# A selective scan, a router, experts and attention on one core: rows read by two kinds of products, unread products placed by a count of work, and a first unit over two queues

## Time and profile before

| | |
|---|---|
| three runs | 1349.19, 1353.96, 1361.01 us (median 1353.96) |
| profiled execution | 1352.84 us, span 1351.4 us |
| mean granted PE clock | 0.875 |
| busy | PE 1197.1 (89%), DVE 781.7 (58%), ACT 513.1 (38%), POOL 314.5 (23%) |
| DVE scans (L1194) | 256, busy 571.5 us |

### The profile page before, as it was taken

One profiled execution on the slowest core, in us unless ns is written; L12 is line 12 of the kernel. 1 busy time (PEld: TensorE's weight loads), 2 busy tenths in 40 slices (PEclk: granted clock), 3 DMA queues, 4 the chain that ended last, 5 costly groups with the idle time before them and its releaser, 6 DMA issues.

```text
span 1351.4 us, 30014 instructions
## 1 busy us (share of the span) xinstructions
PE 1197.1 (89%) x12231; PEld 774.1 (57%) x12231; DVE 781.7 (58%) x926; ACT 513.1 (38%) x1328; POOL 314.5 (23%) x941
## 2 busy tenths in 40 slices
PE   2689898989889899998988499999999598999998
PEld 1555455555545555554554377777777455565665
DVE  5587979699998787978996211121211365542211
ACT  4465556476764655644653111111111111221110
POOL 2043424234334342423323211111111200000000
PEclk9976779589997777957896599999999798999999
DMA  6364846425363153532312562222210300000000
GB/s 177 48 171 88 209 78 157 110 29 139 55 133 69 33 130 45 100 69 48 67 33 91 204 231 99 95 98 94 97 43 16 114 27 0 0 5 11 16 16 16
DMA packets 182202, 110.22 MB, mean 82 GB/s; under 512 B 92285, under 2 KB 176640, under 8 KB 179712
## 3 DMA queue, kind: packets, MB, share of 16 engines
q1 hardware_dynamic: 178176, 99.37, 30.0%
q0 software_dynamic: 3456, 8.48, 1.9%
q10 hardware_dynamic: 432, 0.46, 0.1%
HBM read 63.38 MB, written 43.90 MB: 79 GB/s over the span
## 4 chain that ended last, share of the span: by engine, by line
PE 68%; DVE 13%; ACT 7%; issue 7%; POOL 2%; DMA 2%; SPq 1%; DVEq 0%; POOLq 0%; ACTq 0%
PE psum L1497 10%; PE psum L1509 10%; DVE h L1194 10%; PE psum L2009 8%; PE psum L891 8%; PE psum L877 6%; ACT decay L1026 4%; PE psum L2020 4%; PE psum L858 4%; PE psum L845 3%; PE psum L1952 2%; PE psum L924 2%; PE psum L1944 1%; PE psum L1996 1%; PE psum L901 1%
## 5 line engine op out<-in xcount | busy, mean ns | idle before, releaser
L1194 DVE TENSOR_TENSOR_SCAN h<-decay,psum 128x1024 f32<-128x1024 f32 x256 | 571.5, 2273 | 111.0 <-ACT psum L1036 91.2
L1026 ACT ACTIVATE decay<-psum 128x512 f32<-128x512 f32 x512 | 278.4, 597 | 183.0 <-PE psum L858 181.8
L877 PE MATMUL psum<-xdiag,bstat 96*128 96x64 bf16 x4096 | 199.1, 210 | 17.6 <-DVE h L1194 16.4
L858 PEld LDWEIGHTS psum<-rows,shared 12*128 12x128 bf16 x4096 | 89.9, 103 | 175.5 <-issue 121.8
L877 PEld LDWEIGHTS psum<-xdiag,bstat 96*128 96x128 bf16 x4096 | 165.5, 109 | 38.0 <-DVE h L1194 23.6
L891 PE MATMUL psum<-h,cstat 128*32 128x512 f32 x1024 | 172.8, 756 | 1.2 <-DVE h L1194 1.0
L858 PE MATMUL psum<-rows,shared 12*128 12x64 bf16 x4096 | 123.5, 205 | 23.0 <-DMA rows<-parts_d 14.9
L1497 PE MATMUL psum<-xdt,shared 128*128 128x320 f32 x512 | 141.5, 438 | 0.7 <-ACT xdt L1556 0.7
L1509 PE MATMUL psum<-shared,hid 128*128 128x256 f32 x640 | 139.5, 379 | 0.6 <-ACT hid L1550 0.6
L1353 POOL TENSOR_TENSOR carry<-decay,h 128x16 f32<-128x16 f32 x240 | 58.0, 242 | 335.0 <-ACT decay L1026 334.3
L1509 PEld LDWEIGHTS psum<-shared,hid 128*128 128x128 f32 x640 | 121.0, 190 | 17.2 <-issue 1.1
(11 more groups left out here) (237 smaller groups left out, 1152.6 us busy)
## 6 DMA issues: line engine op xcount, KB each, us to landing
shared<-in_w SPq DMA_DIRECT2D x16, 1024.0 KB, 4.8
xdiag<-x_parts_d SPq DMA_DIRECT2D x128, 96.0 KB
x_parts_d<-x_parts SPq DMA_DIRECT2D x16, 384.0 KB, 3.8
x_parts_d<-x_parts SPq DMA_DIRECT2D x24, 256.0 KB, 3.1
rows<-parts_d SPq DMA_DIRECT2D x128, 48.0 KB
disp_d<-r_xl SPq DMA_DIRECT2D x4, 1305.0 KB, 7.9
xd<-disp_d SPq DMA_DIRECT2D x8, 652.5 KB, 6.3
picked_d<-r_xl SPq DMA_DIRECT2D x4, 1024.0 KB, 5.3
```

What stands on the lines that cost most here:

```text
L858: ins = pe.q.matmul(bank_a[half][:, i * T:(i + 1) * T], s["astat"][strip, RCH * g + q, :], rows[strip, c % 2, q, :], start=True, stop=True)
L877: ins = pe.q.matmul(to.rearrange("p d (s e) -> p s d e", e=2), bstat[0:ROWS, c % 2, b, :], xdiag[0:ROWS, c % 2, b, :, d, :], start=True, s ...
L1026: act.q.activation(decay[:, gi % NB, 8 * half:8 * half + 8, :], per_d(bank_a[half]), ACT.Exp).then_inc(sem("exp"), 1)
L1194: dve.q.tensor_tensor_scan(out=h[:, half_slot(c, half), ch:ch + G, :].rearrange("p d t -> p (d t)"), data0=decay[:, gi % NB, :, :].rearran ...
```

## The change

- `astat`, `rows`: the decay products read all 32 rows of their strip in place of 12. The other 20 rows are zeros, written by two new memsets on POOL in the prologue; the loads of `astat` wait for one, the first `rows` load for the other.
- The input products read 128 rows in place of 96; the upper 32 rows of `bstat` and `xdiag` are zeros that the old memsets write.
- Unread products: `unread_after` counts for each group what PE does beside decays and inputs, in products of 512 columns (`PE_WORK`), and gives each group what it lacks of three. They now multiply `bstat` and `xdiag` (512 columns, 128 rows) from group 2 on: 85 groups get three, 7 get one, 162 none; 262 in all, 48 of them in the first 32 groups.
- 14 unread products after the last router product, and 16 after the last expert product, ahead of the second layer.
- The first unit: A's middle and low parts come ahead of other work on ACT and DVE. SP stores B's parts first. ACT issues the middle and low stores of x, and, after all stores of x have landed, the loads of chunk 0's `xdiag`. SP issues the load of the second unit's tokens between chunk 0's and chunk 1's `rows` loads, no longer in the scan.

```diff
@@ prologue, on_sp
             sp.wait_ge(sem("a_parts_st"), 16)
+            sp.wait_ge(sem("astat_zero"), 1)
             for g in range(ROWG):
...
-            sp.wait_ge(sem("u_dthi"), 1)
-            store_dt(k, s, 0, 0)
-            sp.wait_ge(sem("x_hi"), 1)
-            store_x(k, s, 0, 0)
             sp.wait_ge(sem("u_blo"), 1)
             for j in range(3):
-                store_b(k, s, 0, j)
+                store_b(k, sp, s, 0, j)
+            sp.wait_ge(sem("u_dthi"), 1)
+            store_dt(k, sp, s, 0, 0)
+            sp.wait_ge(sem("x_hi"), 1)
+            store_x(k, sp, s, 0, 0)
             sp.wait_ge(sem("u_dtmid"), 1)
-            store_dt(k, s, 0, 1)
-            sp.wait_ge(sem("u_xmid"), 1)
-            store_x(k, s, 0, 1)
+            store_dt(k, sp, s, 0, 1)
             sp.wait_ge(sem("u_dtlo"), 1)
-            store_dt(k, s, 0, 2)
-            sp.wait_ge(sem("u_xlo"), 1)
-            store_x(k, s, 0, 2)
+            store_dt(k, sp, s, 0, 2)
             sp.wait_ge(sem("bstat_zero"), 1)
-            sp.wait_ge(sem("xdiag_zero0"), 1)
+            sp.wait_ge(sem("rows_zero"), 1)
             sp.wait_ge(sem("st_dt"), DT_ST)
             sp.wait_ge(sem("st_b"), B_ST)
-            load_rows(k, s, 0, LOADS[0])
+            load_rows(k, sp, s, 0, LOADS[0])
+            sp.q.dma_start(ux[:, :, :], x_in[:, UT:2 * UT, :]).then_inc(sem("u_ld"), 16)
+            load_rows(k, sp, s, 1, LOADS[0])
             sp.wait_ge(sem("st_x"), X_ST)
-            load_rows(k, s, 0, LOADS[1] + LOADS[2])
             sp.wait_ge(sem("xdiag_zero1"), 1)
-            load_rows(k, s, 1, sum(LOADS, ()))
+            load_rows(k, sp, s, 1, LOADS[1] + LOADS[2])
@@ prologue, on_pool
             pool.q.memset(s["x_parts"][:, :, :].bitcast(F32), 0.0).then_inc(sem("words_zero"), 1)
+            pool.q.memset(s["astat"][:, :, :].bitcast(F32), 0.0).then_inc(sem("astat_zero"), 1)
             pool.q.memset(s["bstat"][:, :, :, :].bitcast(F32), 0.0).then_inc(sem("bstat_zero"), 1)
+            pool.q.memset(s["rows"][:, :, :, :].bitcast(F32), 0.0).then_inc(sem("rows_zero"), 1)
@@ prologue, on_act
             act.q.copy(x_part[1], s["x_f"]).then_inc(sem("u_xmid"), 1)
+            act.wait_ge(sem("u_xmid"), 1)
+            store_x(k, act, s, 0, 1)
+            act.wait_ge(sem("u_xlo"), 1)
+            store_x(k, act, s, 0, 2)
             act.wait_ge(sem("p_c"), 1)
             act.q.copy(s["cmat"][:, 0, :], bank_c[:, 0:CSPAN]).then_inc(sem("c_taken"), 1)
+            act.wait_ge(sem("xdiag_zero0"), 1)
+            act.wait_ge(sem("st_x"), X_ST)
+            load_rows(k, act, s, 0, LOADS[1] + LOADS[2])
             both_sd(1, late)
@@
+IDLE_ROUTED, IDLE_PLACED = 14, 16
+def unread_products(pe, ident, bank, n):
+    for _ in range(n):
+        pe.q.matmul(bank, ident[:, :], ident[:, :].unsqueeze(1).broadcast_to([P, 4, P]), start=True, stop=True)
...
-AWAKE = (2, 3, 6, 0)
+PE_WORK = {"y": 4, "u_turn": 4, "u_proj": 6, "u_dt": 4, "u_tx": 4, "tr": 2, "yT": 4, "proj": 4}
...
+def unread_after(schedule):
+    work, gi = [0] * (TOTAL + LAG), 0
+    for kind, *x in schedule:
+        if kind == "stream":
+            gi = x[0]
+        elif kind == "y_sel" and x[0] == CHUNKS - 2:
+            break
+        work[gi] += PE_WORK.get(kind, 0)
+    return [max(0, 3 - w) for w in work]
@@ selective_scan, on_pe
-            def stay_awake(bank):
-                pe.wait_ge(sem("tri"), 1)
-                for _ in range(2):
-                    pe.q.matmul(bank, tri[:, 1, :], tri[:, 1, :].unsqueeze(1).broadcast_to([P, 4, P]), start=True, stop=True)
+            def stay_awake(c, n):
+                pe.wait_ge(sem(f"tokens_ld{c % 2}"), TOKENS_LD * (c // 2 + 1))
+                for _ in range(n):
+                    pe.q.matmul(bank_a[1], bstat[:, c % 2, 0, :], xdiag[:, c % 2, 0, 0:2, :, :].rearrange("p k d e -> p (k d e)"),
+                                start=True, stop=True)
...
-                if j in AWAKE and gi > GROUPS * CPB // 4 + 1:
-                    stay_awake(bank_a[1])
+                if gi >= 2:
+                    stay_awake((gi - 1) // GROUPS, unread[gi - 2])
...
-                        strip = slice(32 * g, 32 * g + PAIR_ROWS)
+                        strip = slice(32 * g, 32 * (g + 1))
...
-                        ins = pe.q.matmul(to.rearrange("p d (s e) -> p s d e", e=2), bstat[0:ROWS, c % 2, b, :],
-                                          xdiag[0:ROWS, c % 2, b, :, d, :], start=True, stop=True)
+                        ins = pe.q.matmul(to.rearrange("p d (s e) -> p s d e", e=2), bstat[:, c % 2, b, :],
+                                          xdiag[:, c % 2, b, :, d, :], start=True, stop=True)
...
+            unread_products(pe, ident, bank_y, IDLE_ROUTED)
@@ second_layer, on_pe
         pe.wait_ge(sem("w_rest"), all_weights)
+        pe.wait_ge(sem("evac7"), k.products[7])
+        unread_products(pe, ident, bank_kv[1], IDLE_PLACED)
```

More of the change, by code:

```diff
@@ L187, with load_rows @@
 LOADS = ((("dt", 0), ("dt", 1), ("dt", 2), ("dt", 3), ("b", 0), ("b", 1)), (("x", 0), ("x", 1)), (("x", 2), ("x", 3)))
-def load_rows(k, s, c, piece):
+def load_rows(k, q, s, c, piece):
     buf, t = c % 2, slice(c * T, (c + 1) * T)
@@ L198, in load_rows, with store_dt @@
             src = s["parts_d"][:, :, RCH * n:RCH * (n + 1), t].rearrange("k h p t -> (k h) p t")
-            k.sp.q.dma_start(s["rows"][32 * n:32 * n + PAIR_ROWS, buf, :, :], src).then_inc(rows_ld, 16)
+            q.q.dma_start(s["rows"][32 * n:32 * n + PAIR_ROWS, buf, :, :], src).then_inc(rows_ld, 16)
         elif what == "x":
-            k.sp.q.dma_start(s["xdiag"][2 * PAIR_ROWS * n:2 * PAIR_ROWS * (n + 1), buf, :, n].rearrange("r b d e -> r b (d e)"),
+            q.q.dma_start(s["xdiag"][2 * PAIR_ROWS * n:2 * PAIR_ROWS * (n + 1), buf, :, n].rearrange("r b d e -> r b (d e)"),
                              x_src[n]).then_inc(x_ld, 16)
         else:
-            k.sp.q.dma_start(s["bstat"][n:ROWS:DH, buf, :, STATE * n:STATE * (n + 1)], b_src).then_inc(x_ld, 16)
+            q.q.dma_start(s["bstat"][n:ROWS:DH, buf, :, STATE * n:STATE * (n + 1)], b_src).then_inc(x_ld, 16)
 ROWS_LD, TOKENS_LD = 16 * ROWG, 16 * (S // 2 + DH)
 B_ST, DT_ST, X_ST = 16 * 3, 16 * 5, 16 * 5
-def store_dt(k, s, u, j):
+def store_dt(k, q, s, u, j):
     m, n = MOVED[j]
@@ L215, in store_dt, with store_b, store_x @@
     if n == 1:
-        k.sp.q.dma_start(s["parts_d"][m, :, :, t].rearrange("h p t -> p h t"), s["dt_parts"][j]).then_inc(k.sem("st_dt"), 16)
+        q.q.dma_start(s["parts_d"][m, :, :, t].rearrange("h p t -> p h t"), s["dt_parts"][j]).then_inc(k.sem("st_dt"), 16)
         return
     for dh in range(DH):
-        k.sp.q.dma_start(s["parts_d"][m:m + n, dh, :, t].rearrange("m p t -> p m t"),
+        q.q.dma_start(s["parts_d"][m:m + n, dh, :, t].rearrange("m p t -> p m t"),
                          s["dt_parts"][j][:, dh, :].unsqueeze(1).broadcast_to([P, n, UNIT])).then_inc(k.sem("st_dt"), 16)
-def store_b(k, s, u, j):
+def store_b(k, q, s, u, j):
     m, n = MOVED[j]
     dst = s["b_parts_d"][UNIT * u:UNIT * (u + 1)].rearrange("(i p) m n -> p i m n", p=P)
-    k.sp.q.dma_start(dst[:, :, m:m + n, :], s["b_parts"][:, :, 0:n, :]).then_inc(k.sem("st_b"), 16)
-def store_x(k, s, u, j):
+    q.q.dma_start(dst[:, :, m:m + n, :], s["b_parts"][:, :, 0:n, :]).then_inc(k.sem("st_b"), 16)
+def store_x(k, q, s, u, j):
     m, n = MOVED[j]
@@ L234, in store_x @@
     if n == 1:
-        k.sp.q.dma_start(dst[:, :, m, :], s["x_words"][j]).then_inc(k.sem("st_x"), 16)
+        q.q.dma_start(dst[:, :, m, :], s["x_words"][j]).then_inc(k.sem("st_x"), 16)
         return
     for i in range(2):
-        k.sp.q.dma_start(dst[:, i, m:m + n, :], s["x_words"][j][:, i, :].unsqueeze(1).broadcast_to([P, n, 2 * D])
+        q.q.dma_start(dst[:, i, m:m + n, :], s["x_words"][j][:, i, :].unsqueeze(1).broadcast_to([P, n, 2 * D])
                          ).then_inc(k.sem("st_x"), 16)
@@ L350, in on_act @@
             act.q.copy(a_part[0], a_sb[:, :, :]).then_inc(sem("a_hi"), 1)
+            act.wait_ge(sem("a_rest"), 1)
+            act.q.copy(a_part[1], a_rest[:, :, :]).then_inc(sem("a_mid"), 1)
             act.wait_ge(sem("p_delta"), 1)
             act.q.copy(s["delta"], bank_delta[:, 0:UNIT]).then_inc(sem("p_delta_out"), 1)
-            act.wait_ge(sem("a_rest"), 1)
-            act.q.copy(a_part[1], a_rest[:, :, :]).then_inc(sem("a_mid"), 1)
             act.wait_ge(sem("p_b"), 1)
@@ L430, in on_dve @@
             dve.q.tensor_tensor(a_rest[:, :, :], a_sb[:, :, :], a_part[0], ALU.subtract).then_inc(sem("a_rest"), 1)
-            dve.wait_ge(sem("x_ld_late"), 32)
-            moments(range(UT, 6))
             dve.wait_ge(sem("a_mid"), 1)
@@ L435, in on_dve @@
             dve.q.tensor_tensor(a_part[2], a_rest[:, :, :], a_part[1], ALU.subtract).then_inc(sem("a_lo"), 1)
+            dve.wait_ge(sem("x_ld_late"), 32)
+            moments(range(UT, 6))
             dve.wait_ge(sem("b_hi"), 1)
@@ L554, in unit_steps @@
 def unit_steps(u):
```

(15 more changed lines are left out.)

## The result

The changed kernel takes **1272.84 us** (median of 4 runs, 1271.40 to 1277.38) where the kernel before takes 1357.49 (4 runs, 1349.19 to 1369.98): ratio 0.9401, 95% interval 0.9342 to 0.9461. The forecast was 1254 us, range 1238 to 1290. Ratios and intervals, here and in the table, take only runs within 1.5% of the fastest of the same kernel (of these eight, 1369.98 us stands outside), while medians take all of them, so that a ratio isn't the quotient of the two medians. The profiled execution is the slowest of the four, 1277.38 us with a span of 1276.0.

What follows compares the result with a forecast made beforehand. In the scan, DVE bounds at full clock and PE at half clock. Gains 84.0 - 5 + 5.5 + 12 + 3.5 = 100 us off the profiled 1352.84 give 1252.8; with 1.1 for the median, 1254 us, range 1238 to 1290.

Steps and rivals of the forecast that it cites:

- The rows count: PE's clock: products count with their rows, zeros included, so wider operands hold it; 0.68 with the ring hidden.
- Wider operands: Decays of 32 rows, inputs of 128, and their two memsets on POOL: cost 0 us.
- From group 32 on: Scan's other 224 groups: 84.0 us gained at full pace, less 5 for unread products and short falls.
- 224 x 2.294: Scan from group 32: 224 groups at the full-clock pace of 2.294 us, taken from 597.8, leaving 84.0 us.
- my allowance of 5 for relapses and the ring: Scan from group 32: 2 us for unread products, decays and exponentials waiting in turn, 3 for short clock falls.
- the 515 that I named as a sign: Sign that the forecast holds: the stretch from group 32 to the scan's end takes near 515 us.
- The first 32 groups: Start of the scan, 94.5 us: gain 5.5 from the earlier ux load and 12 of 15.6 from the clock.
- The start: Before the first scan: reordered stores and loads gain 3.5 us, bounds 0 and 5.
- The idle stretches: Unread products before experts and second layer: gain 0, bound 3 us each, as the clock falls again before work.
- Loop: Rival, 0.12: clock holds, but three unread products, decays and exponentials set their groups' pace; 13.6 us, total 1266.
- A: Rival, 0.13: rows don't count, only the unread products' placing works; half the low time stays, total 1297 us.
- C: Rival, 0.05: slower; groups with y products from 32 on lose the pair ahead, clock stays low, 1536 us.

Runs made afterwards that it cites:

- e2: Changed kernel with decays of 12 rows and inputs of 96 again, unread products in the new places: 1422.94 us, ratio 1.044 to the kernel before.
- e4: Changed kernel without unread products in the scan; wide operands and the idle stretches' products stay: 1275.34 us, ratio 0.944 to the kernel before.
- f4: Changed kernel with astat's memset halved, first unit on SP's queue, old unread pairs in the scan, none in the idle stretches: 1269.23 us.
- e5: Changed kernel with the memset of astat in two halves, the second behind DVE's first operations: 1273.11 us, ratio 0.937 to the kernel before.
- f3: The changed kernel measured again, unaltered, in a later batch: 1276.82 us, ratio 0.940 to the kernel before.
- e1: Changed kernel with wide rows kept but the scan's unread products in their old places: 1270.06 us, ratio 0.941 to the kernel before.
- f2: Changed kernel with astat's memset halved, first unit on SP's queue, and the scan's unread products in their old places: 1265.94 us, ratio 0.931.
- f1: Changed kernel with astat's memset in two halves and the first unit on SP's queue alone: 1268.30 us, ratio 0.933 to the kernel before.
- e7: Changed kernel with the first unit's x stores and xdiag loads back on SP's queue, which also reorders them: 1274.23 us, ratio 0.938.
- e6: Changed kernel without the 14 and 16 unread products in the two idle stretches: 1282.84 us, ratio 0.943 to the kernel before.

## Why the prediction was right, and where it was off

The direction, the mechanism and the range held; the profiled execution was put at 1252.8 us and took 1277.38, 24.6 more. By its own steps:

**The rows count (weakest link, 0.68): right, and shown.** e2 without them is slower than before; e4 keeps the gain with no unread product in the scan, f4 with the old pairs. Added rows of zeros count: no product got more numbers that aren't zero. The rule of the Trainium skill ("TensorE: Matmul & The Clock Gate", "What's actually happening"), by which the gate follows how busy the array has been, doesn't tell e2 from the changed kernel if busy is read as time: PE was 98% busy at 0.50 in e2's stretch and 81% busy (436.25 of 535.90; some 85% with the unread products that have no record) at 0.99 in the changed kernel's.

**Wider operands, 0 us: right for PE, wrong for the memsets.** I looked only at whether POOL would be done in time. The memset holds up those of DVE's `TENSOR_SCALAR`s that read and write SBUF: +3.7 us (`uxn` at 13.21 instead of 9.53), shown by e5. The Trainium skill ("SBUF — State Buffer", "SBUF: two separate sides") has it: DVE and GpSimd share a pair of ports, held for a whole instruction, and the other blocks fully. It names which DVE operations need the pair, and the trace agrees: the `TENSOR_TENSOR`s at 6.66 and 6.85, with two inputs against a memset that reads nothing, took 0.16 us in the midst of it. So does a `TENSOR_SCALAR` that reads PSUM: `uxn` took 0.54 us in the kernel before and here, where POOL was clearing `xdiag` beside it (12.15 to 15.81 us).

**From group 32 on, 84.0 less 5: measured 62.0.** This is the largest miss, 17 us, and the failed step is "224 x 2.294". The 2.294 us came from 48 groups in which DVE had 1.49 us of other work and 2.43 of idle time; for 224 groups that makes 6.9 and 11.3. The whole stretch has 17.9 of other work (515.87 less the 497.93 of its 224 scans) and 20.0 idle: 11.0 and 8.7 more, and the scans' own pace adds 2.4 (497.93 against 224/48 of 106.18): 22 us, of which my allowance of 5 for relapses and the ring took off its part. The routing, which that sample hardly held, lies elsewhere in the scan. Of the kernel before, the row of the whole stretch shown above had DVE busy 518.25 us: whatever the clock did, the stretch could not come out much under that. My sum (597.8 less 79.0, 518.8) left 0.6 us for all idle time, and the 515 that I named as a sign left less than none; it doesn't follow from the sum either. Of the 20 us of idle time, 14 gaps are over 0.4 us, and ten of them stand ahead of the seventh scan of an odd chunk, some 3 us after PE has begun on the transposes of a finished tile besides y; two others follow the routing's two table loads on ACT, here those ahead of the gap of 1.65 us that ends at 410.47:

```profile
405.60 1.28 ACT L1185 ACT_TABLE_LOAD   x1
406.89 0.30 ACT L1185 ACTIVATE r_sd<-r_mom,eps 128x4 f32<-128x4 f32 x1
407.20 1.28 ACT L1186 ACT_TABLE_LOAD   x1
```

**The first 32 groups, 17.5 of 94.5: measured 15.5 in this execution and 17.6 in f3.** The second scan came 3.15 us after the first instead of 7.75, waiting for PE, not POOL. The size is right, but by luck in part, for one reason was wrong: I had counted on "48 unread products" to bring the clock up here. The kernels without any in these groups take 72.8 to 77.8 us (e4, e1, f2, f4), those with them and the wide rows 76.6 to 79.0, and the scans' idle time after the first is 2.3 to 6.7 us there against 5.3 to 7.0 in the changed kernel, f1 and f3. So they brought nothing that can be seen here, and may cost a few us.

**The start, -3.5: measured +3.5.** Three parts: the memsets +3.7 to 4.0, the two queues with their order of issues +2.2 (e7), and the reordering, which gained 2.6 (f1, with both taken out: 37.6 against 40.2). The lower bound, "0 (the ACT queue eats all)", was not low enough: I had excluded a loss without a reason for it.

**The idle stretches, 0: measured -3.3 in the experts.** The failed term is the price of an unread product there, "0.22 to 0.31" us at full clock and 0.5 at half; it was 0.87 at full clock, and 14.70/14 = 1.05 over the first stretch. I had read bf16 products, and these multiply a float32 tile. So they last nearly until the work comes, and the fall that I expected ahead of it doesn't come in the first stretch; in the second it came in this execution with the work (1000.2 us) and in most others not. In the second layer the gain of 1 to 4 us (e6, f4) was not to be seen in the first profile.

**Rivals.** Loop: as good as no. The ten gaps at the seventh scan of an odd chunk do stand at groups whose decays have three unread products ahead of them, such as this one, whose decays are those at 302.86 us in the chain shown above:

```profile
307.97 4.70 DVE L1226 TENSOR_TENSOR_SCAN h<-decay,psum 128x1024 f32<-128x1024 f32 x2 [1.16 <-ACT psum L1068]
```

But the gaps are there without the three as well: at these ten scans the idle time is 12.9 us in the changed kernel (10.6 in f3) and 7.9 in e4, which has no unread products in the scan; this one is 0.56 us there. At all other groups with three from group 32 on, 60 of them, it is 0.8 us together. So the ring costs some 3 to 5 us where the finished tile is turned and next to nothing elsewhere, not the 13.6 of this rival; I had taken 2. The sign named for the loop, scans that wait for ACT in groups with three, is there, at that price. Without the threes (e1, e4, f2, f4) the stretch takes 532.0 to 538.4 us, within 4 of the changed kernel. A: no; that "only the placing works" is contradicted by e2. C: without the rows the change is slower, 1.044 in place of 0.940; that the lost pairs are the reason isn't shown apart from the new operands. Its price, 1536, was for the clock staying low throughout; it came back up for 192 of the 687 us. The signs named ahead: clock at 9 from the third slice on (the first has no records), scans' idle time 31.8 (near 30) and no wait for POOL came true, and 0.50 at the end of the second idle stretch in this execution; 515 us, the first scan at 36 to 37 us and 0.50 at the end of the first idle stretch did not. The 214 unread products can't be counted, as a third of them has no record.

The errors leaned one way: 17.0 us (from group 32), 7.0 (start) and 2.0 (first groups) more than forecast, against 1.4 less in the stages behind the scan.

## What to carry to other kernels

Where a clock rises with the work, price the change by the engine that is left as the bound, and take its busy time over the **whole** stretch; a pace from the cleanest sample leaves out the work that comes seldom. A zeroing on POOL isn't free because POOL is idle: look at what DVE runs during it. Padding rows of an operand with zeros costs PE nothing here, and where PE is held at its lower clock while nearly always busy, try it before adding unread products, which then may be left out.

## What the hardware showed that I had not expected

- PE was at 1.2 GHz for 190 us while busy 98% of them (e2), and at 2.4 GHz while busy 81 to 85% with the same schedule over wider rows. Either the decays at 32 rows or the inputs at 128 were enough: 30.7 to 37.5 us low, against 495 with neither.
- A `TENSOR_SCALAR` of 2 elements on DVE took 2.50 us instead of 0.16 while POOL ran a memset of 8192; a `TENSOR_TENSOR` of 2 elements beside the same memset took 0.16.
- With x's stores and the load of `xdiag` on a second DMA queue, the last store of dt took 4.45 us instead of 3.02 and the first scan came 2.2 us later (e7, one execution each).
- 95.6 us at the lower clock in falls of 3.4 to 10.3 us cost the scan 2.6 us against the changed kernel and 6.4 against f4 (e4); before, 239 us in falls of up to 38 cost some 60.
